# Layer norms of a two-block graph network moved to ScalarE as scale and shift, and the copy of x1 moved to a DMA

## What is computed

```
x = layernorm(x + relu(concat(x, adj_norm @ x) @ W0 + b0))          # block 0; its result is x1
# block 1: five layers of a gated graph network on h, starting from h = x1
A = (adj != 0)
for l in range(5):
    agg = A^T @ (h @ W[l])
    h = gru_cell(agg, h)
x = layernorm(x1 + h * mask)
layernorm(x) = (x - mean(x)) / sqrt(var(x) + 1e-5)                  # over the 128 features
```

## Time and profile before

| | |
|---|---|
| time, median of 3 runs | 680.66 us (679.27 to 681.64) |
| span of the profiled execution | 678.2 us |
| PE busy | 621.9 us (92%) |
| DVE busy | 568.8 us (84%) |
| ACT busy | 416.0 us (61%) |
| POOL busy | 390.5 us (58%) |
| mean granted clock of PE | 0.984 |

### The profile page before, as it was taken

The page is one execution under the profiler, slowest core; times in us unless marked ns, Lnnn a source line. Parts: engine busy times, 40 slices in busy tenths (PEclk is TensorE's granted clock), DMA queues, the critical chain, the costliest instruction groups (busy, mean ns, idle before and its releaser), DMA issues.

```text
span 678.2 us, 10100 instructions
## 1 busy us (share of the span) xinstructions
PE 621.9 (92%) x2922; PEld 496.0 (73%) x2922; DVE 568.8 (84%) x1153; ACT 416.0 (61%) x775; POOL 390.5 (58%) x309
## 2 busy tenths in 40 slices
PE   4588899999999999999999999999999999999973
PEld 3467677787877778787777878777787878778852
DVE  1867877989899898989989898998989899886664
ACT  3557385766757576675757667575766667555431
POOL 3526373664757566475767657566765747546252
PEclk9799999999999999999999999999999999999987
DMA  7351302221212222221222221131222111000001
GB/s 226 132 163 40 116 17 78 79 78 51 104 31 84 86 77 77 69 86 31 96 75 77 77 84 71 31 113 57 77 77 92 62 31 62 15 0 16 1 16 31
DMA packets 37424, 47.28 MB, mean 70 GB/s; under 512 B 1409, under 2 KB 18945, under 8 KB 37409
## 3 DMA queue, kind: packets, MB, share of 16 engines
q1 hardware_dynamic: 36368, 46.27, 20.5%
q10 hardware_dynamic: 944, 0.72, 0.3%
q0 software_dynamic: 96, 0.10, 0.2%
HBM read 42.90 MB, written 4.19 MB: 69 GB/s over the span
## 4 chain that ended last, share of the span: by engine, by line
PE 57%; DVE 28%; issue 9%; ACT 4%; DMA 2%; DVEq 1%; POOLq 0%; SPq 0%; ACTq 0%
PE ps_tok L1001 8%; PE ps_tok L1006 7%; DVE edges L733 5%; PE ps_tok L888 4%; DVE r_hn L874 3%; PE ps_r L893 3%; PE ps_r L894 3%; PE ps_b L894 3%; PE ps_b L893 3%; PE ps_r L895 3%; PE ps_b L895 3%; PE ps_z L893 3%; PE ps_z L895 3%; PE ps_z L894 3%; DVE zm_n L807 3%
## 5 line engine op out<-in xcount | busy, mean ns | idle before, releaser
L485 POOL TENSOR_TENSOR h_lo<-h,h_hi 128x512 fp32r<-128x512 f32 x64 | 84.2, 1315 | 108.2 <-ACT h_hi L522 108.2
L495 POOL TENSOR_TENSOR z_h<-z_gate,h 128x512 f32<-128x512 f32 x80 | 104.8, 1310 | 47.2 <-ACT z_gate L645 47.2
L438 POOL TENSOR_TENSOR adjt_lo<-adjt_in,adjt_hi 128x512 fp32r<-128x512 f32 x64 | 95.1, 1508 | 31.3 <-ACT adjt_hi L522 31.3
L1001 PE MATMUL ps_tok<-edges,tok_hi 128*128 (+1 forms) x320 | 92.2, 411 | 17.7 <-DVE edges L733 15.3
L522 ACT ACTIVATE tok_hi<-ps_tok 128x512 fp32r<-128x512 f32 x64 | 38.3, 599 | 108.6 <-PE ps_tok L888 108.5
L573 ACT ACTIVATE n_gate<-n_pre,gru_bias 128x512 f32<-128x512 f32 x80 | 57.7, 722 | 63.4 <-DVE n_pre L774 63.4
L1006 PE MATMUL ps_tok<-edges,tok_lo 128*128 (+1 forms) x320 | 88.4, 399 | 0.0
L1001 PEld LDWEIGHTS ps_tok<-edges,tok_hi 128*128 128x128 f32 x320 | 59.0, 191 | 38.7 <-issue 22.9
L829 DVE TENSOR_TENSOR h<-z_h,zm_n 128x512 f32<-128x512 f32 x80 | 85.2, 1065 | 0.8
L807 DVE SCALAR_TENSOR_TENSOR zm_n<-z_gate,n_gate 128x512 f32<-128x512 f32 x80 | 66.2, 828 | 22.1 <-ACT n_gate L573 20.1
L874 DVE SCALAR_TENSOR_TENSOR r_hn<-ps_hn,gru_bias,r_gate 128x512 f32<-128x512 f32 x80 | 59.5, 744 | 27.2 <-ACT r_gate L635 27.0
(11 more groups left out here) (123 smaller groups left out, 1603.3 us busy)
## 6 DMA issues: line engine op xcount, KB each, us to landing
adjt_in<-in_adj_t_dram SPq DMA_DIRECT2D x16, 1024.0 KB, 5.2
adj_in<-in_adj_dram SPq DMA_DIRECT2D x16, 1024.0 KB, 5.2
xt_in<-in_x_t_dram SPq DMA_DIRECT2D x16, 256.0 KB, 2.8
x_in<-in_x_dram SPq DMA_DIRECT2D x16, 256.0 KB, 2.7
out_dram<-y_out SPq DMA_DIRECT2D x16, 256.0 KB, 2.3
wl_t<-in_wl_t_dram ACTq DMA_DIRECT2D x1, 320.0 KB, 5.4
wih_t<-in_w_ih_t_dram ACTq DMA_DIRECT2D x1, 192.0 KB, 3.0
whh_t<-in_w_hh_t_dram ACTq DMA_DIRECT2D x1, 192.0 KB, 9.3
```

The costliest lines, as they stand in the source:

```text
L438: nc.gpsimd.tensor_tensor(adjt_lo[:, j, :], adjt_in[:, j, :], raw(adjt_hi[:, j, :]), ALU.subtract).then_inc(s_adjt_lo, 1)
L485: nc.gpsimd.tensor_tensor(h_lo[made][:], h[made][:], raw(h_hi[made][:]), ALU.subtract).then_inc(s_h_lo, 1)
L495: nc.gpsimd.tensor_tensor(z_h[:], z_gate[:], h[layer][:], ALU.mult).then_inc(s_zh, 1)
L1001: nc.tensor.matmul(ps_tok[:], tok_hi[:, c * P:(c + 1) * P], edges_from(c, unit[0]), start=c == 0, stop=False)
```

## The change

1. ACT now applies both norms: one activation (Identity) for each of the four 128x128 column blocks computes scale * x + shift, with scale = rstd and shift = -mean * rstd, both one value per partition.
2. DVE makes the shifts: one 128x4 instruction for shift1 in the place of its four L709, and one for shift2 in slot 3 (slot 2 in window 17) ahead of zm_n.
3. ACT's four for x1 stand in slot 4 between n_gate and agg_hi (in windows -1, 0 and 1 ahead of the rounding of x1, behind agg_hi). ACT's four for y_out stand in slot 3 (slot 2 in window 17) behind the rounding of the turned state (tok_hi) and ahead of h_hi and r_gate.
4. POOL keeps rstd1 and rstd2, and no longer makes cent2 and y_out. It no longer waits for the store ahead of rstd2; ACT waits for it ahead of y_out.
5. The copy x1 to x1_kept is no ACT instruction any more but a DMA from SBUF to SBUF, issued by SP between the load of x and the load of adj, when x1 is complete. ACT waits for the landing of the copy before it overwrites x1 in the next window, DVE waits for it ahead of pre2 three windows on.
6. DVE waits, before it overwrites pre1 and pre2, for the ACT instructions that read them.

```diff
@@ sync
+                    if w.finishes():
+                        sp.wait_ge(s_end_read, w.finished(1, 1))
+                    sp.wait_ge(s_x1, w.prepared(C, C))
+                    sp.dma_start(x1_kept[:, bass.ds(kept, 1), :, :].rearrange("p o c d -> p (o c d)"),
+                                 x1[:].rearrange("p c d -> p (c d)")).then_inc(s_x1_kept, 16)
@@ gpsimd, last_norm
-                    pool.wait_ge(s_stored, w.freed(16))
                     pool.wait_ge(s_var2, w.finished(1, 1))
                     nc.gpsimd.tensor_tensor(rstd2[:], var2[:], minus_half[:], ALU.pow).then_inc(s_rstd2, 1)
-                    nc.gpsimd.tensor_tensor(cent2[:], pre2[:], mv2[:, :, 0:1].to_broadcast([P, C, D]),
-                                            ALU.subtract).then_inc(s_cent2, 1)
-                    nc.gpsimd.tensor_tensor(y_out[:], cent2[:],
-                                            rstd2[:].rearrange("p (c o) -> p c o", o=1).to_broadcast([P, C, D]),
-                                            ALU.mult).then_inc(s_out, 1)
@@ scalar
+                def norm1():
+                    act.wait_ge(s_shift1, w.prepared(1, 1))
+                    if w.first >= 0:
+                        act.wait_ge(s_x1_kept, w.prepared(16, 0))
+                    for c in range(C):
+                        nc.scalar.activation(x1[:, c, :], pre1[:, c, :], ACT.Identity, bias=shift1[:, c:c + 1],
+                                             scale=rstd1[:, c:c + 1]).then_inc(s_x1, 1)
+                def norm2():
+                    act.wait_ge(s_stored, w.freed(16))
+                    act.wait_ge(s_shift2, w.finished(1, 1))
+                    for c in range(C):
+                        last = nc.scalar.activation(y_out[:, c, :], pre2[:, c, :], ACT.Identity,
+                                                    bias=shift2[:, c:c + 1], scale=rstd2[:, c:c + 1])
+                    last.then_inc(s_out, 1)
...
+                    if w.prepares() and slot == 4 and not w.ramps():
+                        norm1()
                     if w.unit(slot):
                         act.wait_ge(s_agg, w.units(slot + 1))
                         evacuate(agg_hi[:], ps_tok[:]).then_inc(s_agg_hi, 1)
...
+                            if w.ramps():
+                                norm1()
                             act.wait_ge(s_x1, w.prepared(C, C))
                             evacuate(tok_hi[:], x1[:].rearrange("p c d -> p (c d)")).then_inc(s_x1_hi, 1)
-
-                            evacuate(x1_kept[:, bass.ds(kept, 1), :, :].rearrange("p o c d -> p (o c d)"),
-                                     x1[:].rearrange("p c d -> p (c d)")).then_inc(s_x1_kept, 1)
                     if w.next_turned(slot):
                         v, s = w.next_turned(slot)
                         act.wait_ge(s_tok, v.turned(s + 1))
                         evacuate(tok_hi[:], ps_tok[:]).then_inc(s_tok_hi, 1)
+                    if w.finishes() and w.first < B + 2 and slot == w.out_slot():
+                        norm2()
@@ vector, norm1
-                    for c in range(C):
-                        nc.vector.tensor_scalar(x1[:, c, :], pre1[:, c, :], mv1[:, c, 0:1],
-                                                rstd1[:, c:c + 1], ALU.subtract, ALU.mult).then_inc(s_x1, 1)
+                    nc.vector.scalar_tensor_tensor(out=shift1[:], in0=mv1[:, :, 0], scalar=-1.0, in1=rstd1[:],
+                                                   op0=ALU.mult, op1=ALU.mult).then_inc(s_shift1, 1)
```

More of the change, by code:

```diff
@@ L102, in end_slot, with out_slot @@
         return 2 if self.batches - 1 <= self.first < self.batches + 1 else 1
+    def out_slot(self):
+        return 2 if self.idles() else 3
     def idles(self):
@@ L243, in program @@
         rstd1 = sb("rstd1", [P, C])
+        shift1 = sb("shift1", [P, C])
         x1 = sb("x1", [P, C, D])
@@ L264, in program @@
         rstd2 = sb("rstd2", [P, C])
-        cent2 = sb("cent2", [P, C, D])
+        shift2 = sb("shift2", [P, C])
         y_out = sb("y_out", [P, C, D])
@@ L306, in program @@
         s_rstd1 = sem("s_rstd1")
+        s_shift1 = sem("s_shift1")
         s_x1 = sem("s_x1")
@@ L342, in program @@
         s_rstd2 = sem("s_rstd2")
-        s_cent2 = sem("s_cent2")
+        s_shift2 = sem("s_shift2")
         s_out = sem("s_out")
@@ L388, in window @@
             def window(w):
+                if w.prepares():
+                    kept = sp.snap(w.batch(-1) % KEPT)
                 if w.loads():
@@ L396, in window @@
                 if w.finishes():
-                    sp.wait_ge(s_out, w.finished(1, 1))
+                    sp.wait_ge(s_out, w.finished(1, 2))
                     sp.dma_start(out[w.batch(3)].rearrange("(c p) d -> p c d", p=P), y_out[:]).then_inc(s_stored, 16)
@@ L403, in window @@
                     load_x(b)
+                if w.prepares():
+                    if w.finishes():
[3 more added lines that the diff above has]
+                                 x1[:].rearrange("p c d -> p (c d)")).then_inc(s_x1_kept, 16)
+                if w.loads():
+                    b = w.batch(-2)
                     sp.wait_ge(s_row_sum, w.prepared(C, C))
@@ L419, in _ @@
         def _(pool):
-            pool.sem_inc(s_cent2, 1)
             nc.gpsimd.memset(zeros[:], 0.0).then_inc(s_const, 1)
@@ L446, in last_norm @@
                 def last_norm():
-                    pool.wait_ge(s_stored, w.freed(16))
                     pool.wait_ge(s_var2, w.finished(1, 1))
                     nc.gpsimd.tensor_tensor(rstd2[:], var2[:], minus_half[:], ALU.pow).then_inc(s_rstd2, 1)
-                    if w.first == B + 2:
-                        return
-                    nc.gpsimd.tensor_tensor(cent2[:], pre2[:], mv2[:, :, 0:1].to_broadcast([P, C, D]),
-                                            ALU.subtract).then_inc(s_cent2, 1)
-                    pool.wait_ge(s_rstd2, w.finished(1, 1))
-                    pool.wait_ge(s_cent2, w.finished(1, 2))
-                    nc.gpsimd.tensor_tensor(y_out[:], cent2[:],
-                                            rstd2[:].rearrange("p (c o) -> p c o", o=1).to_broadcast([P, C, D]),
-                                            ALU.mult).then_inc(s_out, 1)
                 for slot in range(SLOTS):
@@ L511, in _ @@
         def _(act):
+            act.sem_inc(s_out, 1)
             act.wait_ge(s_const, 2)
@@ L562, in h0_hi_of_batch @@
                     evacuate(h_hi[0][:], h[0][:]).then_inc(s_h0_hi, 1)
-                if w.prepares():
-                    kept = act.snap(w.batch(-1) % KEPT)
+                def norm1():
[12 more added lines that the diff above has]
+                    last.then_inc(s_out, 1)
                 for slot in range(SLOTS):
@@ L707, in norm1, with norm2 @@
                     dve.wait_ge(s_rstd1, w.prepared(1, 1))
-                    for c in range(C):
-                        nc.vector.tensor_scalar(x1[:, c, :], pre1[:, c, :], mv1[:, c, 0:1],
-                                                rstd1[:, c:c + 1], ALU.subtract, ALU.mult).then_inc(s_x1, 1)
+                    nc.vector.scalar_tensor_tensor(out=shift1[:], in0=mv1[:, :, 0], scalar=-1.0, in1=rstd1[:],
+                                                   op0=ALU.mult, op1=ALU.mult).then_inc(s_shift1, 1)
+                def norm2():
+                    dve.wait_ge(s_rstd2, w.finished(1, 1))
+                    nc.vector.scalar_tensor_tensor(out=shift2[:], in0=mv2[:, :, 0], scalar=-1.0, in1=rstd2[:],
+                                                   op0=ALU.mult, op1=ALU.mult).then_inc(s_shift2, 1)
                 def residual():
@@ L715, in residual @@
                     dve.wait_ge(s_mixed, w.prepared(1, 1))
+                    if w.first >= 0:
+                        dve.wait_ge(s_x1, w.prepared(C, 0))
                     nc.vector.scalar_tensor_tensor(out=pre1[:], in0=mixed[:], scalar=0.0, in1=x_in[:],
@@ L738, in pre2_of_batch @@
                     dve.wait_ge(s_last, w.finished(1, 1))
-                    dve.wait_ge(s_x1_kept, w.finished(1, 1))
-                    dve.wait_ge(s_cent2, w.freed())
+                    dve.wait_ge(s_x1_kept, w.finished(16, 16))
+                    dve.wait_ge(s_out, w.freed())
                     b = w.batch(3)
```

## The result

The changed kernel takes 723.95 us against 681.07 us: a ratio of 1.0645 (95% interval 1.0624 to 1.0666), 6.5% slower. The forecast was 715.0 with a range of 697 to 729. The profiled execution has a span of 722.3 us, 44.1 more than before.

A forecast was written before the change was run, and what follows sets the result against it. The prediction took an ACT-DVE relay in slots 3 and 4 as the limit: 12 windows of 2.51 + 0.10 us plus the ends gave +34.3, span 712.5, and 2.5 on top 715.0 us; own range 706 to 722, wider 697 to 729.

The forecast's parts named there:

- The price of an activation: Each new 128x128 ACT instruction takes 0.48 us and occupies 0.38 with overlap; bounds 0.20 and 0.48 occupied.
- (a): shift2 on DVE in slot 3, ahead of zm_n, lies on the chain to agg_lo: +0.10 us a window.
- (b): norm2 on ACT in slot 3, between tok_hi and r_gate, makes r_gate and those behind it 1.32 us late.
- (c): norm1 on ACT in slot 4 ahead of agg_hi: agg_hi 2.51 us late, 1.32 from norm2 and 1.19 from norm1.
- (d): DVE without L709 saves 1.44 less 0.10 us, worth 0 because agg_lo then waits for agg_hi.
- (e): From agg_hi's end to the edges' end 4.84 us stay, so the edges end 2.51 us later.
- The race of tok_lo and h: Port contest behind agg_hi: tok_lo ready after 0.59 us, h after 0.64; if h wins, edges gain 0 to 0.6.
- (f): POOL without cent2 and y_out, ACT without x_kept: room gained where nobody waited, worth 0.
- (g): The DMA of x1 lands in about 2.3 us with most of a window to spare: 0, even at four times that.
- the clock: Rival: PE's clock falls behind the L1001 stall, up to 3.4 us a window, 756 us, or 735 in half; chance 0.08.
- dear activations: Rival: new ACT instructions cost 0.48 us each with nothing overlapping, agg_hi +3.4, 727 us; chance 0.07.
- faster: Rival: ACT's norms delay agg_hi in slot 4 by less than 0.29 us, agg_lo comes 0.29 earlier, 677 us; chance 0.04.

The follow-up runs named there:

- e7: Changed kernel with ScalarE's last norm ahead of tok_hi in slot 3 and its norm of x1 behind agg_hi in slot 4: 683.09 us.
- e8: Changed kernel with the norm of x1 on ScalarE moved behind agg_hi and the last norm back on GpSimd: 682.23 us.
- e5: Changed kernel with one move: ScalarE's last norm ahead of tok_hi in slot 3 in place of behind it: 701.30 us.
- e1: Changed kernel with only the norm of x1 on ScalarE (ahead of agg_hi), the last norm back on GpSimd: 702.38 us.
- e11: Kernel before the change with only the low part of x1 (tok_lo) on VectorE behind the edges in windows 2 to 14: 677.23 us.
- e9: Kernel of e8 with the low part of x1 (tok_lo) on VectorE behind the edges in windows 2 to 14: 674.92 us.
- e3: Kernel before the change with only the copy to x1_kept made by DMA in place of ScalarE: 679.69 us.
- e10: Kernel of e9 with the last norm on ScalarE, ahead of tok_hi in slot 3: 675.70 us.
- e6: Changed kernel with one move: ScalarE's norm of x1 behind agg_hi in slot 4 in place of ahead of it: 695.99 us.
- e2: Changed kernel with only the last norm on ScalarE (ahead of r_gate), the norm of x1 back on VectorE: 695.42 us.
- e4: Changed kernel with 8 unused matmuls added on TensorE behind the gates of slot 4 in windows 2 to 14: 714.83 us.

## Why the prediction was right, and where it was off

- *The price of an activation*: 0.48 us, 0.38 with the overlap. Measured 0.480 and 0.482, and four in 1.64. The two ends of the price are both out.
- *(a) shift2, +0.10*: e7 and e8 differ by 0.06, e5 and e1 by 0.09, and PE has a new stall of 0.17 us for agg_lo in slot 3. Right within what can be told.
- *(b) norm2, +1.32*: r_gate 1.34 later. Right; e5 shows that it is the place.
- *(c) norm1, agg_hi 2.51 late in all*: agg_hi 2.17 behind n_gate, forecast 2.14; from slot 3's tok_hi to agg_hi 6.49 us, before 3.96, so 2.53 late. Right.
- *(d) DVE's saving is worth 0*: right here (1.33 us of waiting for agg_hi). Behind agg_hi it shows, and with POOL's row relieved it counts: with the low part on DVE the window is 39.08 with the norm on DVE (e11) and 38.83 with it on ACT (e9). That is read from the windows; the intervals of the two total times overlap.
- *(e) the 4.84 us stay*: 4.83. Window 41.93, forecast 41.9. The three pieces for PE were forecast as 0.8, then up to 1.7 in all, then about 2.2; measured 0.68, 0.55 and 2.01. The race of tok_lo and h went to tok_lo.
- *(f), (g) POOL, x_kept and the transfer are worth 0*: e3 and the pair of e9 and e10 show it, the start-up's later loads included.
- *The sum.* The filled kernel, which leaves the clock out, has a span of 712.0 against a forecast of 712.5. Its parts: the ends behind window 13's load of adj are 122.75 us there and 118.65 before, so 4.1, of which 2.6 are window 14 and 1.5 the tail (forecast 1.4). The eleven windows between give 28.5 (forecast 28.7). Of the start nothing can be said to 0.4 us: up to window 2 it differs by some us between the traces (126.3 in e3, 130.8 in e1), for reasons that stay open. The 2.5 us put on top of the span set a median beside the span of another execution; where both are known of one execution they differ by 1.8 (724.1 and 722.3).
- *The term that was mis-sized is the clock*, which I kept as a rival at 0.08 and which is not in the sum. It was priced as up to 3.4 us a window, from a stretch behind a stall of 3.94 us. It fell in six of the eleven windows and once more behind them (the stretch from window 13's load of adj to the end is 124.24 us, in the filled kernel 122.75), and cost 1.5 us each time, 10.3 in all. That is the whole distance from the span that was forecast (712.5) to the one measured (722.3). The sign named for it came: PE's busy time grew in the long windows.
- *What the chance of 0.08 left out.* It set one fall behind 3.94 us against one stretch (52 to 56 us) without a fall; the stalls about that stretch are at most 1.8 us. The trace of before has more in its start-up, which the prediction did not use: a stall of 2.99 us that ends at 23.76, behind which the clock is at its lower level from 25.7 us on, and one of 3.42 us that ends at 29.11, behind which it stays there up to 31. Waits, timeline and windows view of PE:

```profile
PE ps_b L893 <- DVE xt_lo L661: 3.0, 1, 3.0
...
29.11 1.12 PE L888 MATMUL ps_b<-ident,x 128*128 128x128 f32 x4 [3.42 <-DVE x L709]
...
29.00:33.00 4.00, 3.79 (x12) 0.64 0.42 151
```

So a fall was on record at 2.99 us and none up to 1.8, and the forecast stall of about 2.2 us lay between: the price was open there, and the chance was set too low.

- *That the range held is partly luck.* 723.95 us lies outside the range that I gave as my own (706 to 722). It lies inside 697 to 729, whose upper end was kept for dear activations, and those did not come: the price of an activation was right, and the clock filled the room. Without the clock the forecast of 715.0 is met (714.83 us in the filled kernel).
- The rival *faster* named 0.29 us as the delay of agg_hi from which it decides. The moved kernels are its case, and there POOL took the gain, which neither it nor my expectations for e6 to e8 saw: I had followed tok_lo only to the edges and not through the three POOL instructions behind it, and missed all three by 10 us or more.

## What to carry to other kernels

What an instruction costs on an in-order engine is decided by who stands behind it in the list: the same four activations cost 1.4 us a window ahead of r_gate and 0.1 one wait earlier, where the engine idled anyway. When work is taken off an engine, ask whether that engine was waiting at that point and follow everything that hangs on the moved result to its last reader, on every engine. And where a change lengthens a stall of TensorE by a us, price the clock behind it, from every stall of the trace, the start-up's too; a filler of unused matmuls tells at once whether it matters.

## What was not expected of the hardware

- The granted clock fell to its lower level behind stalls of 2.0 us in six of eleven windows of the changed kernel, in three of eleven of e1 and in two of e5, and once behind a stall of 1.78 us (the changed kernel at 639.9 us: 0.65 in the 4.7 us behind it). Behind stalls of 1.7 us (e2) and 0.6 us (e4) it stayed at 1.00 through the steady stretch, and behind one of 1.78 us in the kernel before (at 56.3 us) too. At the same stall it fell in some windows and not in others, so the length of the stall alone doesn't decide; what else does stays open. That PE's standing still is its cause, the filler shows. The Trainium skill ("TensorE: Matmul & The Clock Gate", Why this matters for your kernels) names idle gaps between bursts of matmuls as what brings the slower clock back; in kind the runs agree, but the gaps it warns of are longer than the 2.0 and 1.78 us measured here, and the measurement decides.
- Taking turns between DVE and POOL goes both ways. Once tok_lo is away from POOL, h_lo there grows from 1.3 to 2.36 us (e11) beside the last edges and DVE's tok_lo, and z_h to 1.75: time taken from h on DVE came back on POOL. The Trainium skill ("SBUF — State Buffer", two separate sides) calls the shared ports an exclusive lock for the whole instruction. These rows agree that one engine stands while the other works; h_lo's 1.06 us more span the work of more than one DVE instruction, so how the turn passes when several follow each other stays open.
